# Eight maxima and a transpose of one phase: from the end of one attention stage to the start of the next

## The reference

```python
x = x + _L0_conv_ref(_gn(x), ...)   # global attention, 12 heads of 16, relative position bias
x = x + _L1_conv_ref(_gn(x), ...)   # 7 x 7 neighbourhood attention plus 16 register keys
```

## Time and profile before

| | us |
|---|---|
| median of 3 runs | 4865.21 |
| lowest, highest | 4857.58, 4866.6 |
| the profiled execution | 4862.39 |
| its span, first to last instruction | 4860.6 |
| PE busy in it | 4446.6 (91%) |
| DVE busy in it | 3079.8 (63%) |
| ACT busy in it | 2594.1 (53%) |

### The profile page before, as it was taken

How to read it: one execution, slowest core, us unless ns; L and a number is a source line. 1 busy time by engine, 2 the same in 40 slices (tenths; PEclk the granted TensorE clock), 3 DMA queues, 4 the chain that set the end, 5 groups by cost and what they waited for, 6 DMA issues and landing times.

```text
span 4860.6 us, 97545 instructions
## 1 busy us (share of the span) xinstructions
PE 4446.6 (91%) x32598; PEld 2268.6 (47%) x32598; DVE 3079.8 (63%) x5558; ACT 2594.1 (53%) x3955; POOL 892.4 (18%) x1901
## 2 busy tenths in 40 slices
PE   4879999999999999999999999999999999999988
PEld 3334453544535454453544535454453544535434
DVE  3736667666675756657566675756757566675644
ACT  1533556555564655555555565555546555565564
POOL 4122021222202222021222202222031221202111
PEclk7988999999999999999999999999999999999999
DMA  6333152442514433153442424433253432424402
GB/s 123 87 73 77 44 119 64 100 87 56 107 42 107 88 89 75 44 115 68 100 80 58 101 52 103 91 83 75 45 114 75 100 80 49 103 60 100 88 15 40
DMA packets 235869, 386.05 MB, mean 79 GB/s; under 512 B 58396, under 2 KB 133728, under 8 KB 235360
## 3 DMA queue, kind: packets, MB, share of 16 engines
q1 hardware_dynamic: 189280, 266.13, 23.7%
q10 hardware_dynamic: 21504, 75.51, 7.8%
q0 software_dynamic: 24576, 37.80, 4.9%
HBM read 227.79 MB, written 88.08 MB: 65 GB/s over the span
## 4 chain that ended last, share of the span: by engine, by line
PE 71%; DVE 11%; issue 6%; DMA 5%; SPq 5%; ACT 2%; DVEq 0%; ACTq 0%; POOL 0%
PE P L1143 14%; PE P L1161 13%; PE P L1102 12%; DVE mx L909 7%; PE P L966 5%; PE P L967 5%; PE P L1193 4%; PE P L1214 4%; DMA queries<-oraw 4%; PE P L1110 3%; PE P L1079 3%; SPq L514 3%; DVE mxc L915 2%; PE P L1186 1%; PE P L1231 1%
## 5 line engine op out<-in xcount | busy, mean ns | idle before, releaser
L909 DVE TENSOR_REDUCE mx<-P 128x1 f32<-128x512 f32 x3072 | 1921.3, 684 | 457.4 <-PE P L1102 453.3
L779 ACT ACTIVATE probs<-P 128x1024 f32<-128x1024 f32 x1536 | 1507.5, 1022 | 854.0 <-PE P L1161 853.8
L1102 PE MATMUL P<-K,AR 96*128 96x256 f16 x6144 | 1074.1, 278 | 56.6 <-DMA AR<-biases 29.5
L1161 PE MATMUL P<-AR,K 113*128 113x512 f16 x3072 | 924.9, 383 | 13.2 <-DMA AR<-mrow 12.6
L915 DVE TENSOR_REDUCE mxc<-P 128x1 f32<-128x336 f32 (+1 forms) x1536 | 656.3, 474 | 317.9 <-PE P L1111 315.0
L1143 PE MATMUL P<-probs,V 128*17 128x512 f32 x6144 | 813.5, 601 | 5.7 <-ACT probs L779 5.7
L1102 PEld LDWEIGHTS P<-K,AR 96*128 96x128 f16 x6144 | 532.2, 98 | 581.4 <-DVE mx L909 202.0
L795 ACT ACTIVATE probs<-P 128x320 f32<-128x320 f32 (+3 forms) x1632 | 612.1, 437 | 338.2 <-PE P L1214 268.4
L1161 PEld LDWEIGHTS P<-AR,K 113*128 113x128 f16 x3072 | 213.3, 98 | 670.3 <-ACT probs L779 519.6
L1110 PE MATMUL P<-K,A 112*128 112x320 f16 (+1 forms) x1536 | 405.2, 300 | 68.7 <-DVE mx L909 54.9
L1214 PE MATMUL P<-A,K 113*128 113x320 f16 (+2 forms) x1536 | 428.3, 300 | 14.7 <-ACT probs L795 14.3
(11 more groups left out here) (125 smaller groups left out, 3718.4 us busy)
## 6 DMA issues: line engine op xcount, KB each, us to landing
AR<-biases SPq DMA_DIRECT2D x384, 256.0 KB, 7.9
AR<-queries ACTq DMA_DIRECT2D x96, 512.0 KB, 5.9
biases<-xn SPq DMA_DIRECT2D x128, 256.0 KB, 2.6
AR<-queries ACTq DMA_DIRECT2D x96, 256.0 KB, 8.8
K<-oraw POOLq DMA_DIRECT2D x384, 64.0 KB, 4.7
xin<-in_x_dram SPq DMA_DIRECT2D x16, 768.0 KB, 10.5
queries<-oraw SPq DMA_DIRECT2D x384, 32.0 KB, 4.6
QA<-queries SPq DMA_DIRECT2D x192, 64.0 KB, 2.8
```

What stands on the lines that cost most here:

```text
L779: nc.scalar.activation(probs[:, u % RING, j:j + 2, :], P[:, b:b + 2, :], ACT.Exp).then_inc(p_done[0], 1)
L909: V_.reduce_max(mx[:, n // 2, n % 2:n % 2 + 1], bank, AX.X).then_inc(used, 1)
L1102: last = mm(bank[:, QD * (v % 2):QD * (v % 2) + QD], AR[0:ROWS_MAX[0], part % SLOTS, v, c, j, 128 * q:128 * q + 128], K0[0:ROWS_MAX[0], h, ...
L1161: last = mm(P[:, j, :], K0[0:ROWS, h, 128 * kt:128 * kt + 128], AR[0:ROWS, p % SLOTS, kt // 2, :, j, :], start=True, stop=True)
```

## The change

The last nine jobs of layer 0's phase 1 (maxima 24 to 31 and the transpose) leave main 1 and the jobs stage of image 1, and stand ahead of phase 2 in the next main 0. The 57 jobs left in main 1 are spread over the same steps 25 to 98; the 42 jobs in main 0 are spread over steps 0 to 21 where 33 lay in steps 0 to 19. Image 0 is as before, and nothing else is changed.

```diff
-THIRD = 16
+THIRD, SECOND = 16, 24
@@ plan_l0
-        placed = evenly(max_jobs(0, image, 2), 0, 20)
+        placed = evenly(max_jobs(0, image, 1)[SECOND:] + max_jobs(0, image, 2), 0, 22)
@@ plan_l1
-    placed += evenly(max_jobs(0, n0, 0) + max_jobs(0, n0, 1), 25, STEPS[1] - TAIL)
+    placed += evenly(max_jobs(0, n0, 0) + max_jobs(0, n0, 1)[:SECOND], 25, STEPS[1] - TAIL)
@@ block_stages
-        yield "jobs", 0, n0, first_phases(n0, *max_jobs(0, n0, 1), *stat_jobs(1, i0))
+        yield "jobs", 0, n0, first_phases(n0, *max_jobs(0, n0, 1)[:SECOND], *stat_jobs(1, i0))
```

## The result

The changed kernel takes 4880.54 us (median of 6 runs, 4873.66 to 4886.21) against 4864.91 for the kernel before (6 runs beside them, 4857.58 to 4875.42). The ratio is 1.0029, with a 95% interval of 1.0016 to 1.0043: 15.6 us slower. Forecast was 4863, no change; the time lies inside the range of 4842 to 4884, on its slower side.

What follows compares the result with a forecast made beforehand. PE looked the bound over the whole span, with DVE nearly full too in mid main 1. Main 1's 14 x 4.2 plus 6.5 less main 0's 15 x 4.2 gained 2.3 us: about 4863, no change, range 4842 to 4884.

Steps and rivals of the forecast that it cites:

- Main 1 from step 25 on: Main 1: nine jobs less and the transpose's idle time gone give 4.2 us per pass, bounds 2.7 and 5.4.
- Image 1's jobs stage: Paced by DVE alone; eight reductions less and a statistics job covered give 6.5 us once, 3.5 as lower end.
- steps 14 to 17, no low stretch there: Main 0: one job more each at steps 14 and 17, ahead of position-bias jobs; 0.7 us, 0.4 to 1.2.
- steps 18, 19: Main 0: four wide maxima instead of two, beside four narrow ones and the transpose; 0.4 us more, 0.3 to 0.7.
- steps 20, 21: Main 0: two maxima and phase 2's transpose join three narrow maxima; 1.8 us more, between 1.5 and 2.1.
- the unit of steps 94 to 97: End of main 1: without the transpose PE no longer waits for DVE; 3.69 to 2.31, 1.38 us gained.
- the shorter pitch: DVE reductions stand 0.60 to 0.61 us apart, not the whole instruction length of 684 ns.
- The sum: Whole kernel: 14 x 4.2 + 6.5 - 15 x 4.2 = 2.3 us gained, so about 4863; chance 0.52.
- the bounds: Whole kernel: all term bounds at their ends give 38 us gained or 47 lost; range taken 4842 to 4884.
- DVE pacing main 1: First rival, main 1: every job taken out gives back 0.60 us; 19 us faster, 4846; chance 0.27.
- The start of main 0 as the bound: Second rival, main 0 steps 14 to 21: crowding costs 5.5 us per image; 17 slower, 4882; chance 0.16.
- The tail not relieved: Third rival, end of main 1: PE's stand stays, main 1 gains only 2.8 us; 17 slower, 4882; chance 0.05.

Runs made afterwards that it cites:

- e1: Kernel before with eight dummy matmuls of 512 columns ahead of each position-bias job of main 1; 4971.17 us.
- e2: Changed kernel with eight dummy matmuls of 512 columns ahead of each position-bias job of main 1; 4983.43 us.
- e9: Changed kernel with few dummy matmuls in main 1: two ahead of each first-group bias job, six and one in the second; 4870.03 us.
- e10: Kernel before with few dummy matmuls in main 1: two ahead of each first-group bias job, six and one in the second; 4869.20 us.
- e3: Changed kernel with its 42 jobs of main 0 spread over steps 0 to 26 instead of 0 to 21; 4875.10 us.
- e7: Kernel before with two more matmuls at step 40 of main 0, 0.43 us per image, 7 us in all; 4879.09 us.
- e8: Kernel before with four more matmuls at step 40 of main 0, 14 us in all; 4886.93 us.
- e12: Changed kernel with two more matmuls at step 40 of main 0, 0.43 us per image, 7 us in all; 4879.10 us.
- e4: Kernel before with its 33 jobs of main 0 spread over steps 0 to 26 instead of 0 to 19; 4878.20 us.

## Why the prediction was right and wrong

**Right: the sum of the moved work.** Main 1 from step 25 on gave 64.0 / 14 = 4.6 us per pass where 4.2 were forecast; main 0 cost 64.5 / 15 = 4.3 ahead of step 36 where 4.2 were forecast, and 2.4 / 15 = 0.16 behind it. At the full clock they are 4.44 and 4.03. Image 1's jobs stage gave 6.1 us where I said 6.5, with 3.5 as the lower end. That end rested on the clock's rise staying where it was; it came earlier (403.2, 400.8 and 406.3 us in the three profiles of after, against 409.4 to 410.3), along with the stage, as the Trainium skill's page "TensorE: Matmul & The Clock Gate", Part 1, would have it.

**Right: most units.** Medians over the passes, forecast and measured change in us:

| unit of main 0 | forecast | measured |
|---|---|---|
| steps 2, 3 | +0.5 | +0.60 |
| steps 4, 5 | +0.5 | +0.54 |
| steps 8, 9 | +0.3 | +0.43 |
| steps 10, 11 | 0 | -0.03 |
| steps 14 to 17, no low stretch there | +0.7 | +0.63 |
| steps 18, 19 | +0.4 | +0.37 |
| steps 20, 21 | +1.8 | +1.66 |

Steps 0 and 1, which the prediction leaves out, got 0.17 us shorter. Over all passes the median of steps 14 to 17 grew by 1.7 us, as a low stretch falls there in more than half of the passes of after. In main 1 the unit of steps 94 to 97 went from 3.69 to 2.03, and the end from step 98 stayed at 2.01 instead of the 2.19 of the earlier trace rows: ACT was not late there. The pitch of a reduction is still about 0.6 us (24 take 14.44 in the jobs stage of after), so the shorter pitch was the one to use.

**Wrong: all else was taken as unchanged.** The step that failed is "The sum": 14 x 4.2 + 6.5 - 15 x 4.2 counts the stages that the change touches and takes each other stage, and the clock in it, at its old length. Steps 0 to 24 of main 1 hold the same jobs and grew by 0.97 us in each of 14 passes, 13.5 us. With it the sum is -64.0 + 64.5 - 6.1 + 13.5 and some 1.5 of small terms, +9.4, against 9.5 between the profiles. At the full clock the moved work gained 7.8 us, more than the 2.3 forecast; the early part, and the low stretches in main 0, made a loss of it. The timed medians stand 15.6 apart; the runs of one kernel spread over 13 to 18 us, so three profiles and six runs need not agree more closely. All 84 timed runs of the kernel before and the 8 of the changed one have medians 13.4 apart (4865.2, 4878.5). For the 4 to 6 us beyond the profiles there is no trace. The mean granted clock of a run doesn't tell the two kernels apart: at 0.964 the kernel before takes 4868.0 us (mean of the 15 such runs of the study), the changed one 4880.5 (2 runs). That fits with a low stretch costing by its place and not by its length alone.

**Wrong: the bounds.** Each term had bounds but this one had none, though the trace of before shows its size: the same work of steps 0 to 24 takes 25.98 us in one pass and 28.29 in another there. Fourteen passes at either of these would lie 32 us apart. That belonged into the range as a term of its own. The range held the time by luck: its slow end came from rivals that did not happen.

**The rivals.** DVE pacing main 1: a unit of three maxima takes 1.98 to 2.04 us in after, or 1.86 and 1.87 in steps 40 to 43 and 74 to 77, of which the first took 1.87 before too; so no. The start of main 0 as the bound: its price was 4.3 us and 4.0 at the full clock, below the 5.1 from which that rival decides, though the 4.05 us of steps 20 and 21 is its pattern in small. The tail not relieved: it was.

**What stays open.** That the second low stretch and the later landing make up the 13.5 us is shown by the accounts above. That the difference of the early part goes when fillers cover the wait is shown by one profile each of e1, e2, e9 and e10; in the whole time it goes with e9 and e10 only, and with e1 and e2 it stays in doubt. Why the kernel before has the second stretch in 17 of 42 passes and the changed one in 28 is only in part answered: its waits are longer, since its transfer lands later and its first low stretch is a little shorter (4.31 against 4.63 us per pass). Why the transfer lands later is answered one step back. SP issues it, before and after, in the two passes above:

```profile
2079.90 1.71 SPq L478 DMA_DIRECT2D QA<-queries  x4
```
```profile
1209.40 1.72 SPq L478 DMA_DIRECT2D QA<-queries  x4
```

That is 10.50 and 10.90 us into the stage, right behind the landing of the last write of its queries (L514). On the mean of the three profiles this write is issued at 1.9 us in both kernels and lands at 10.61 before and 10.91 after. Why that write takes longer is not answered. SP, ACT and POOL issue all the transfers ahead at the same places of the stage, to 0.05 us, up to the last two that SP issues for the queries; e3, e7, e8 and e12 show the late landing (14.34 to 14.36), e4 and e9 do not (14.12, 14.11). As e7 and e8 leave every job in its place, it is not the moved jobs or their transfers as such.

## What to carry to other kernels

Price a move between stages by neighbouring units of the trace that differ by one job; that gave every term here to a few tenths of a us. Then look at the stages that the change leaves alone: take the same stretch in each pass of the trace before, and where it varies, as here from 26.0 to 28.3 us, put that spread times the number of passes into the range, because a change elsewhere may redeal it. And before believing a result of a few tenths of a per cent, apply one small neutral edit to both kernels and see whether the difference keeps its sign.

## What was not expected of the hardware

- TensorE's clock fell to its lower level in the midst of work: in the pass shown PE was busy 5.95 of the 6.80 us ahead of the fall, most of it in the 64-column matmuls of the bias jobs, and the longest wait was 0.60 us.
- How much a low stretch costs depends on what stands behind it. One of 6.7 us ahead of a wait for a transfer cost next to nothing (the pass took 26.07 us, and the one pass of the three profiles of before without any took 25.76); one of 10.4 us behind that wait made the pass 29.32.
- 0.43 us of work per image, 7 us in all, moved the median by 14 us in one kernel and by -1.4 in the other, though the runs spread too widely to call either apart from 7.
- The same transfers, issued at the same places of a stage, landed 0.3 us later in some kernels than in others, in all three profiles of both the kernel before and the changed one.
